# Gathers between two expert layers: issued in pairs behind a common wait, in place of three in flight

## The reference

```
x = x + attention(layernorm(x))                 # 8 heads
x = x + experts0(layernorm(x))                  # 64 experts, 6 per token, and a shared one
x = x + lookup_attention(layernorm(x))
x = x + experts1(layernorm(x))                  # 8 experts, 2 per token

def experts0(x):                                # T = 2048, D = 128, hidden 96
    scores = sigmoid(x @ gate_w)
    _, topk_idx = top_k(scores + gate_bias, 6)
    topk_w = scores[topk_idx] / (sum + 1e-20) * 2.5
    routed = sum over experts e of mask[:, e] * ((silu(x @ g_e) * (x @ u_e)) @ d_e)
    shared = silu(x @ sh_gate) * (x @ sh_up) @ sh_down
    return routed + shared

def lookup_attention(x):
    w = softmax(x @ W_attn + b_attn);  idx = clip(int(x @ W_off + b_off), 0, 127)
    s = sum(x[:, 0, idx] * w)
    return broadcast(s) @ W_out + b_out
```

## Time and profile before

| what | value |
|---|---|
| timed runs, median | 868.16 us (866.82 to 869.16) |
| profiled execution, span from first to last instruction | 1023.1 us |
| busy: TensorE / VectorE / ScalarE / GpSimd | 740.8 / 604.7 / 498.4 / 425.6 us |
| gathers, first to last start | 593.5 to 712.8 us |
| last expert layer, first to last scatter-add start | 901.6 to 1006.6 us |

### The profile page before, as it was taken

One profiled execution on the slowest core, in us unless ns is written; L12 is line 12 of the kernel. 1 busy time (PEld: TensorE's weight loads), 2 busy tenths in 40 slices (PEclk: granted clock), 3 DMA queues, 4 the chain that ended last, 5 costly groups with the idle time before them and its releaser, 6 DMA issues.

```text
span 1023.1 us, 18229 instructions
## 1 busy us (share of the span) xinstructions
PE 740.8 (72%) x6306; PEld 444.5 (43%) x6309; DVE 604.7 (59%) x1330; ACT 498.4 (49%) x747; POOL 425.6 (42%) x659
## 2 busy tenths in 40 slices
PE   5799999899889777338899960300377677599992
PEld 3322222222223222138899930200245543399992
DVE  5899998898889755446676410000265766244442
ACT  4788888778777645213444421000344432165550
POOL 4310023522442345366677667776002033345553
PEclk9999999999999878659999995655675776699997
DMA  8999999999992000528866522222000010133346
GB/s 254 249 286 288 283 273 280 288 276 291 310 358 105 19 25 31 129 87 245 258 191 171 157 54 52 54 52 51 0 11 14 19 33 32 37 37 49 48 51 138
DMA packets 83482, 142.96 MB, mean 140 GB/s; under 512 B 10736, under 2 KB 75728, under 8 KB 81888
## 3 DMA queue, kind: packets, MB, share of 16 engines
q1 hardware_dynamic: 57744, 118.07, 40.4%
q0 software_dynamic: 12784, 17.40, 7.8%
q10 hardware_dynamic: 12864, 6.33, 2.3%
HBM read 116.57 MB, written 101.34 MB: 213 GB/s over the span
## 4 chain that ended last, share of the span: by engine, by line
PE 53%; another core or an unknown queue 14%; DVE 9%; ACT 9%; issue 6%; DMA 5%; SPq 2%; POOL 1%; DVEq 0%; POOLq 0%; ACTq 0%
PE PS L664 11%; PE PS L650 8%; PE PS L1010 6%; PE PS L639 6%; DMA XP<-slots_scratch 3%; ACT PB L1146 3%; PE PS L1020 3%; PE PS L802 3%; PE PS L789 2%; PE PS L791 2%; ACT PB L1149 2%; PE PS L777 2%; PE PS L849 1%; ACT PS L1141 1%
## 5 line engine op out<-in xcount | busy, mean ns | idle before, releaser
L1679 DVE TENSOR_SCALAR PS<-PS 128x1024 f32<-128x1024 f32 x241 | 288.1, 1229 | 55.4 <-PE PS L639 30.1
L1146 ACT ACTIVATE PB<-PS 128x1024 f32<-128x1024 f32 x192 | 194.5, 1025 | 52.6 <-PE PS L650 46.0
L664 PE MATMUL PS<-PB,VS 128*32 128x256 f32 x2048 | 168.5, 402 | 3.4 <-issue 3.3
L639 PE MATMUL PS<-QS,KP 64*128 64x512 bf16 (+1 forms) x640 | 101.2, 347 | 38.1 <-ACT PB L1149 18.7
L1393 POOL DMA_INDIRECT slots_scratch<-XN,slot x96 | 93.3, 972 | 61.1 <-ACT PB L1146 36.5
L1453 POOL DMA_INDIRECT GB<-y_scratch,slotc x96 | 90.9, 946 | 37.1 <-issue 29.4
L650 PE MATMUL PS<-QM,KP 64*128 64x512 bf16 (+1 forms) x640 | 102.3, 350 | 3.5 <-DVE PS L1679 3.4
L838 PE MATMUL PS<-wshd,OH 96*128 96x128 f32 x64 | 11.7, 356 | 111.6 <-DVE OH L1820 110.7
L1463 POOL DMA_INDIRECT slots_scratch<-XN,slot x32 | 32.0, 1000 | 140.8 <-DVE slot L1964 130.8
L1483 POOL DMA_INDIRECT sums_scratch<-YO,XG x39 | 60.6, 1555 | 60.9 <-DVE YO L2034 59.7
L1149 ACT ACTIVATE PB<-PS 128x1024 f32<-128x1024 f32 x64 | 64.7, 1026 | 40.5 <-PE PS L650 26.8
(11 more groups left out here) (297 smaller groups left out, 1411.5 us busy)
## 6 DMA issues: line engine op xcount, KB each, us to landing
y_scratch<-YP SPq DMA_DIRECT2D x80, 128.0 KB, 2.5
slots_scratch<-slots_scratch SPq DMA_DIRECT2D x1, 8768.0 KB
W0GU<-in_w0gu SPq DMA_DIRECT2D x1, 6144.0 KB, 50.1
XP<-slots_scratch ACTq DMA_DIRECT2D x80, 64.0 KB, 2.8
XP<-slots_scratch SPq DMA_DIRECT2D x80, 64.0 KB, 2.7
W1GU<-in_w1gu SPq DMA_DIRECT2D x8, 512.0 KB, 4.1
W0D<-in_w0d SPq DMA_DIRECT2D x1, 3072.0 KB
XG<-slots_scratch SPq DMA_DIRECT2D x39, 68.5 KB
```

The source lines that it names most:

```text
L639: last = mm(o, keys, QS[g][r, x], start=first, stop=True, skip_group_check=not first)
L664: last = mm(PS[32 * j:32 * j + 32, at:at + HALF], VS[:, n, g * HG + j, :], PB[u // 2 % 3][:, 2 * (j % 2) + j // 2, q], start=(n == 0 and h ...
L1146: A(PB[u // 2 % 3][:, 2 * hp:2 * hp + 2, :], pair_banks(u).rearrange("p (j q) -> p j q", j=2), ACT.Exp).then_inc(sem("exp_done"), 1)
L1679: TS_(pair_banks(u), pair_banks(u), 4.0, 0.0, ALU.mult, ALU.max).then_inc(sem("relu_done"), 1)
```

## The change

The number of semaphores goes from three to two. A gather with an even number (from 2 on) waits for both gathers of the pair before it, and a gather with an odd number waits for nothing. TensorE's wait in line 848 and ScalarE's in line 1211 follow the two semaphores. Line numbers of the changed kernel are one higher from here on.

```diff
-        IN_FLIGHT = 3
+        IN_FLIGHT = 2
...
                 for n in range(first, last):
                     t, k = 4 * q + n // TOP0, n % TOP0
                     g = TOP0 * t + k
-                    if g >= IN_FLIGHT:
-                        pool.wait_ge(sem(f"gathered{g % IN_FLIGHT}"), 16 * (g // IN_FLIGHT))
+                    if g >= IN_FLIGHT and g % IN_FLIGHT == 0:
+                        for i in range(IN_FLIGHT):
+                            pool.wait_ge(sem(f"gathered{i}"), 16 * (g // IN_FLIGHT))
                     gp.indirect_dma_start(GB[:, t, k, :], None, y0_dram.rearrange("b p d -> (b p) d"),
                                           bass.IndirectOffsetOnAxis(ap=slotc[:, t, k:k + 1], axis=0)).then_inc(
                                               sem(f"gathered{g % IN_FLIGHT}"), 16)
```

## The result

The changed kernel takes 951.14 us (median of 4 runs, 947.67 to 952.35), the kernel before 868.66 us beside it (866.82 to 869.87). The ratio is 1.0952, 95% interval 1.0929 to 1.0975: slower by 82.5 us. The forecast was 942 us with a range of 911 to 963.

A forecast was written before the change was run, and what follows sets the result against it. Gathers, waited for in pairs of 4.335 us, were to bound every chunk; the last chunk starts 73.4 us later, so 868.16 + 73.4 = 941.6, say 942 us, range 911 to 963.

The forecast's parts named there:

- The 155 us between the trace and the timed runs: Profiled span 1023.1 us against 868.16 timed: the gather stage's TensorE stall was taken as little or not in timed runs.
- its sum of 855 us: Whole kernel: 1023.1 us less 112.0 of gather-stage stall, 28 of other releaserless waits and 28 of idle wait.
- What the pair costs: GpSimd's gathers: each pair takes 1.255 + 2.33 + 0.75 = 4.335 us, where it cost 2.51.
- The restart: GpSimd, from a pair's landing to the next pair's first gather: 0.75 us, with 0.27 as the other end.
- the landing: A gather's time from start to landed data, taken as 2.33 us.
- What was hidden: Gathers beside lookups: last gather lands 85.6 us later, last chunk starts 73.4 later; dispatches of the first two chunks stay hidden.
- The cover: Slack of the last gather before the last chunk's lookup: some 12 us, used up by the later gathers.
- Cheap restart: Rival at the pair's wait: restart 0.27 us, a pair 3.855 us, last chunk +50.8 us, 919 us; chance 0.19.
- The stall broken by pauses: Rival in the gather stage: timed runs have the stall and pauses break it, 38.6 us less, 830 us; chance 0.05.
- no difference: Rival: lookups begin so late in timed runs that 86 us of later gathers are hidden, 868 us; chance 0.04.
- Worse by slower descriptors: Rival at the gathers: descriptors take longer beside working VectorE, and lookups are shorter, 951 to 963 us; chance 0.10.
- The prediction's sign for TensorE: Sign of being right: TensorE at line 849 waits for GB in each of the first three lookups.

The follow-up runs named there:

- the second trace: The kernel before, unchanged, traced again: 868.02 us, ratio 0.9996.
- the order of the waits: The changed kernel with its two waits asked for in the other order, so that the DMA itself carries gathered1: 927.66 us, ratio 1.0674.
- the depth of two pairs: The changed kernel with four semaphores, each pair waiting for the pair two back, up to four gathers in flight: 870.73 us, ratio 1.002.
- groups of three: The changed kernel with IN_FLIGHT = 3, three gathers behind a common wait for the three before: 924.09 us, ratio 1.0651.

## Why the prediction was right, point by point

**The 155 us between the trace and the timed runs.** Right: the second trace has no stall, a first lookup at 34.8 us after the first gather (34.5 forecast: 628.0 - 593.47) and 100.8 us from the first lookup to the last (102.3 forecast). Between first gather and first lookup it is 111.7 us shorter than the first trace (112.0 forecast). Ahead of the first gather it is 46.3 us shorter (593.47 - 547.14), where the prediction took off 28 and 28; its sum of 855 us is therefore some 10 us below the traced 864.5. The forecast of the change doesn't rest on that sum. Too general was the sentence that TensorE's completions come late for as long as gathers run one behind the other: in the second trace they run so, 1.25 us apart, and nothing is late.

**What the pair costs.** The step was right, and decided by experiment (the order of the waits, the depth of two pairs); its size was small by 0.19 us: 4.52 in place of 4.335. The restart was 0.74 (0.75 forecast), the second gather started 1.24 to 1.25 us after the first (1.255). The term that was mis-sized is the landing. The prediction read 2.33 us off the window in which the first gather's packets end; the waiting engine sees the landing 2.5 us after the start, some 0.2 us behind that window's end. (The first trace has no row with a gather's landing; the second has, 2.4/2.5/3.3.) Over 47 pairs 0.19 us is 8.8 us, and forecast and result are 9.1 us apart. The estimate of 2.15 us from the Trainium skill ("DMA: Bandwidth & Descriptors", section "Anatomy of one DMA — SWDGE (gpsimd) path") would have been 0.35 us short of the measured 2.5 for a gather.

**What was hidden.** Right within 2.4 us of cover: the last gather landed 85.6 us later by the forecast and, at 764.38 + 2.43 - 550.56 = 216.3 against 122.4 us, 93.9 us later in the traces; 84.1 us of that reached the last lookup. The cover was 9.8 us, 12.2 in the forecast (85.6 - 73.4). The dispatches of the first two chunks began at 765.63 and stayed off the path.

**The rivals.** Cheap restart was decided by which wait the DMA carries, as the order showed: with the waits exchanged it is true, at 927.66 us. The stall broken by pauses had nothing to break, and no late start of the lookups was there to hide the gathers (no difference): the first lookup is at 34.8 us. Worse by slower descriptors didn't come: the gathers beside a working VectorE took 942 ns at the median, 944 in the second trace of before. Of whole gathers held for as long as a VectorE copy runs, which the prediction draws from the Trainium skill's rule on the shared port ("SBUF — State Buffer", section "Who interferes with whom"), no run here shows any. Single gathers were longer, one of 96 in the changed kernel (last section).

The prediction's sign for TensorE came: in the changed kernel its products of line 849 waited for gathers 52 times, 67.5 us in all, before the first lookup and during each but the last; in the second trace of before 4 times, 2.5 us, all ahead of the first lookup. Windows of the same stage, before (second trace) and after; length, busy time of PE, PEld, DVE, ACT, POOL (xcount), granted clock, DMA share, GB/s:

```profile
616.00:646.00 30.00, 22.43 (x97) 15.10 (x97) 19.92 (x77) 12.28 (x33) 22.68 (x25) 0.67 0.22 60
646.00:676.00 30.00, 20.93 (x97) 13.51 (x96) 22.21 (x93) 10.82 (x27) 22.68 (x25) 0.71 0.22 63
```

```profile
640.00:690.00 50.00, 29.04 (x104) 18.46 (x104) 22.95 (x93) 13.98 (x36) 20.85 (x23) 0.56 0.10 29
690.00:740.00 50.00, 29.18 (x100) 18.41 (x99) 20.65 (x86) 13.08 (x34) 20.77 (x22) 0.51 0.13 36
```

GpSimd is busy 22.68 of 30 us before and 20.8 of 50 after, with about as many indirect DMAs in each stretch (25, and 22 or 23; all gathers, but for the last seven of the second stretch before, which are dispatches): the same work, spread over 5/3 of the time.

## What to carry to other kernels

A wait costs what is still on its way when the engine gets there: before adding one, subtract the age of the youngest transfer it looks at from the landing time, and if the result is positive, multiply it, with the restart, by the number of waits (here 2.5 - 1.25 + 0.74 = 1.99 us, 47 times). What other work covers, 9.8 us here, comes off once. Limit transfers in flight by waiting for the one several places back, not for the last; if several waits stand before one instruction, list them so that the instruction itself carries the one that comes last. And where a trace's span is far from the timed runs, find the stretch that can hold the difference before summing anything from it, or trace again.

## What the runs showed of the hardware that was not expected

- The order of two waits ahead of an indirect DMA on GpSimd: 0.26 us from the landing to the next start if the DMA carries the late one, 0.70 if an instruction ahead of it does; 23.5 us of 951.14 here.
- In one execution of an unchanged program TensorE's completions came late, with 115 us of waits in three pieces while indirect DMAs ran back to back; nine further traces of the same stage, one of the same program, had none of it: ScalarE's waits for line 827 add up to 9 to 19 us there. Its cause was not found.
- TensorE's granted clock fell with its waiting: 0.67 and 0.71 in two windows of the lookups before, 0.56 and 0.51 after, between its two levels of 0.5 (1.2 GHz) and 1.0 (2.4 GHz). In a stage that gathers bound this cost little: the eight products of line 890 ahead of the last lookup took 1.52 us at a granted clock of 0.50, eight of the same line 31 us later 1.07 at 1.00.
- A gather that GpSimd starts while VectorE adds two 128x512 f32 operands, both from SBUF, can take longer by most of what is left of that addition. In the changed kernel one did, 1.29 us in place of 0.94, beside an addition that had 0.46 us to go:

```profile
629.66 0.69 DVE L1912 TENSOR_TENSOR PR<-PR 128x512 f32<-128x512 f32 x1
```

```profile
629.89 1.29 POOL L1454 DMA_INDIRECT GB<-y_scratch,slotc  x1 [0.30 <-issue]
```

All eleven gathers of over 1.1 us in the ten traces started beside such an addition (lines 1905 and 1911 of the kernel before); one that started beside 0.72 us of it took no longer (groups of three, 0.94 us). No run moved the additions, so that they are the cause is not shown; in the sum it is nothing.
